# Wv products split by head into 64-column halves, and the first batch's qk splits moved

## The reference, cut to what matters

```python
q = (xn @ w_q).reshape(B, SQ, 16, 64)
k, v = jnp.split(context @ w_kv, 2, axis=-1)
scores = jnp.einsum('bqhd,bkhd->bhqk', q * SCALE, k)
attn = jax.nn.softmax(scores, axis=-1)
out = jnp.einsum('bhqk,bkhd->bqhd', attn, v).reshape(B, SQ, 1024)
out = out @ w_out + b_out
```

## Time and profile before

| | us |
|---|---|
| median of 3 runs | 995.58 |
| lowest, highest | 993.61, 996.96 |
| the profiled execution's time | 992.81 |
| its span | 991.0 |
| PE busy in the span | 942.5 (95%) |
| PE weight loads busy | 815.2 |
| DVE busy | 741.7 |
| ACT busy | 502.8 |
| POOL busy | 561.3 |
| mean granted TensorE clock | 0.993 |

### The profile page before, as it was taken

How to read it: one execution, slowest core, us unless ns; L and a number is a source line. 1 busy time by engine, 2 the same in 40 slices (tenths; PEclk the granted TensorE clock), 3 DMA queues, 4 the chain that set the end, 5 groups by cost and what they waited for, 6 DMA issues and landing times.

```text
span 991.0 us, 17563 instructions
## 1 busy us (share of the span) xinstructions
PE 942.5 (95%) x5732; PEld 815.2 (82%) x5732; DVE 741.7 (75%) x1167; ACT 502.8 (51%) x856; POOL 561.3 (57%) x593
## 2 busy tenths in 40 slices
PE   6898999999999999999999999999998699999998
PEld 3467898888988889888888888998886587888887
DVE  5549787787877878778777887865776666888776
ACT  3447556655565556556555655654452343434432
POOL 5719678668948957876894795720000431444440
PEclk9999999999999999999999999999999799999999
DMA  5872112212211212221221121101004022222200
GB/s 159 274 232 71 45 55 62 56 42 59 63 38 53 71 36 59 60 59 38 60 66 39 47 69 41 54 4 64 1 1 170 1 85 86 86 85 85 85 1 22
DMA packets 75094, 66.50 MB, mean 67 GB/s; under 512 B 7920, under 2 KB 71680, under 8 KB 75008
## 3 DMA queue, kind: packets, MB, share of 16 engines
q1 hardware_dynamic: 75008, 65.37, 21.9%
HBM read 57.48 MB, written 7.86 MB: 66 GB/s over the span
## 4 chain that ended last, share of the span: by engine, by line
PE 83%; DVE 10%; issue 3%; ACT 2%; POOL 2%; DMA 0%; SPq 0%; POOLq 0%; DVEq 0%; ACTq 0%
PE sps L1205 26%; PE scp L1223 9%; PE scp L1224 9%; PE scp L1225 9%; PE scp L1413 5%; PE sps L1399 5%; PE wps L1399 4%; PE wps L1249 3%; PE scp L1414 2%; DVE u_sb L916 2%; DVE st L881 1%; PE sps L1316 1%; PE scp L1173 1%; PE sps L1336 1%; PE sps L1159 1%
## 5 line engine op out<-in xcount | busy, mean ns | idle before, releaser
L1223 PE MATMUL scp<-cn,pt_hi 128*128 128x258 f32 (+1 forms) x832 | 239.7, 288 | 3.6 <-DVE pt_lo L906 2.8
L1224 PE MATMUL scp<-cn,pt_hi 128*128 128x256 f32 (+1 forms) x832 | 234.9, 282 | 0.7 <-issue 0.7
L1225 PE MATMUL scp<-cn,pt_lo 128*128 128x258 f32 (+1 forms) x832 | 234.9, 282 | 0.0
L668 ACT ACTIVATE st<-sps 128x512 f32<-128x512 f32 (+1 forms) x208 | 123.1, 594 | 155.9 <-PE sps L1205 155.1
L906 DVE TENSOR_TENSOR pt_lo<-st,pt_hi 128x512 fp32r<-128x512 f32 (+1 forms) x208 | 194.7, 936 | 6.6 <-ACT pt_hi L677 6.6
L881 DVE TENSOR_TENSOR st<-st,mbc 128x512 f32<-128x512 f32 (+1 forms) x208 | 156.9, 754 | 44.7 <-ACT mbc L691 37.5
L1205 PE MATMUL sps<-qk_hi,ct_hi 128*128 128x512 f32 (+1 forms) x416 | 167.9, 404 | 17.7 <-DVE cmax L892 7.4
L674 ACT ACTIVATE st<-st 128x512 f32<-128x512 f32 (+1 forms) x208 | 130.2, 626 | 93.5 <-DVE st L881 92.7
L1223 PEld LDWEIGHTS scp<-cn,pt_hi 128*128 128x128 f32 (+1 forms) x832 | 156.9, 189 | 13.8 <-DVE pt_lo L906 5.7
L1205 PE MATMUL sps<-qk_hi,ct_lo 128*128 128x512 f32 (+1 forms) x416 | 164.2, 395 | 0.0
L1205 PE MATMUL sps<-qk_lo,ct_hi 128*128 128x512 f32 (+1 forms) x416 | 163.4, 393 | 0.0
(11 more groups left out here) (213 smaller groups left out, 1481.4 us busy)
## 6 DMA issues: line engine op xcount, KB each, us to landing
w_raw<-W SPq DMA_DIRECT2D x16, 1024.0 KB, 7.5
raw<-ctx_t SPq DMA_DIRECT2D x96, 128.0 KB, 2.2
raw<-ctx_n SPq DMA_DIRECT2D x96, 128.0 KB, 2.0
raw<-qk_scratch SPq DMA_DIRECT2D x56, 128.0 KB, 2.0
qk_scratch<-stage_b SPq DMA_DIRECT2D x4, 896.0 KB, 4.6
qk_scratch<-stage_a SPq DMA_DIRECT2D x4, 896.0 KB, 4.5
wq_sb<-w_q SPq DMA_DIRECT2D x1, 1024.0 KB, 5.1
wkt_sb<-w_kt SPq DMA_DIRECT2D x1, 1024.0 KB, 8.0
```

What stands on the lines that cost most here:

```text
L668: act.activation(st[0:rows(j), par, j, :], sps[0:rows(j), u % 2, :], ACT.Copy).then_inc(out_ok, 1)
L1223: pe.matmul(scp[:, t, 0:D + 2], hi, cn[0:rows(j), j, 0:D + 2], start=j == 0, stop=False)
L1224: pe.matmul(scp[:, t, 0:D], hi, cn[0:rows(j), j, D + 2:CNW], start=False, stop=False)
L1225: ins = pe.matmul(scp[:, t, 0:D + 2], lo, cn[0:rows(j), j, 0:D + 2], start=False, stop=j == SJ - 1)
```

## The change

`times_wv` does one product per head and half of the features instead of one for two heads: 64 columns of Wv against that head's 64 columns of u. Head 0's result lands on partitions 0 to 63, head 1's on 64 to 127, both in the same 64 columns of PSUM, so `take_o` is one copy of 128 partitions x 256 instead of two of 64 x 256.

In the first batch `first_high` and `first_low` of tiles 0 to 3 now stand before `q_high` and `q_low` of the next q tile instead of behind them; those of tiles 4 to 7 stand one slot later, behind the next slot's work.

```diff
@@ ScalarE (VectorE the same, with first_low and q_low)
             for t in range(GT):
                 take_qk(t)
+                first_high(t)
                 q_high(GT + t)
-                first_high(t)
@@
                 slot(0, u, u)
                 if u in LATE_TILE:
                     take_qk(LATE_TILE[u])
-                    first_high(LATE_TILE[u])
+                if u - 1 in LATE_TILE:
+                    first_high(LATE_TILE[u - 1])
@@ VectorE, take_o
-                v = wps[:, 0, :].rearrange("p (t q) -> p t q", t=GT)
-                dve.tensor_copy(oT[0:Q, ts_, tok], v[0:Q, :, 0:Q])
-                dve.tensor_copy(oT[Q:P, ts_, tok], v[Q:P, :, Q:P]).then_inc(o_ok, 1)
+                dve.tensor_copy(oT[:, ts_, tok],
+                                wps[:, 0, 0:GT * Q].rearrange("p (t q) -> p t q", t=GT)).then_inc(o_ok, 1)
@@ TensorE, times_wv
                     for dt in range(DT):
-                        ins = pe.matmul(wps[:, 0, t * P:(t + 1) * P], wv_sb[:, dt, h0:h0 + P], ut_sb[:, t, dt, :],
-                                        start=dt == 0, stop=dt == DT - 1)
+                        for hr in head_rows:
+                            ins = pe.matmul(wps[hr, 0, t * Q:(t + 1) * Q],
+                                            wv_sb[:, dt, h0 + hr.start:h0 + hr.stop], ut_sb[:, t, dt, hr],
+                                            start=dt == 0, stop=dt == DT - 1)
```

More of the change, by code:

```diff
@@ L868, in _ @@
                 take_qk(t)
+                first_low(t)
                 q_low(GT + t)
-                first_low(t)
             def rows(j):
@@ L948, in _ @@
                     take_qk(LATE_TILE[u])
-                    first_low(LATE_TILE[u])
+                if u - 1 in LATE_TILE:
+                    first_low(LATE_TILE[u - 1])
             with dve.Fori(0, NPASS - 1) as i:
```

## The result

The changed kernel takes 981.35 us (median of 4 runs, 980.75 to 982.35) against 994.6 us for the kernel before on the same chip (4 runs). The ratio is 0.9872 with a 95% interval from 0.9854 to 0.9889: 13.2 us less. The forecast was 11.5 us less and 984.1 us, with a range of 976.5 to 999. Of the 2.7 us between forecast and result, 1.0 come from the kernel before, whose median is 994.6 over four runs where three had given 995.6; 1.7 are gain that the sum did not have. The profiled execution has a span of 979.0 us, 12.0 less than before.

The account below looks back on a forecast made before the run. TensorE was taken to bound the kernel, except in the first batch, where VectorE and ScalarE steps hold it. Gains 1.6 + 2.5 + 7.4 = 11.5 us, so 995.6 - 11.5 = 984.1 us; range 976.5 to 999.

Parts of the forecast that it names:

- Wv: Each group's Wv products on TensorE go from 1.79 to 1.33 us, 7.4 us less in 16 groups.
- the shape: Entering and leaving column halves around a group's Wv products costs 0.40 us, bounds 0 and twice that.
- main term: Wv products: two heads on different column halves load and multiply at the same time, 7.4 us less in 16 groups.
- staggered in program order: Wv starts: one head's first instruction runs beside the other's second, so four instructions take 116 ns.
- take_o: VectorE's single copy saves 0.42 us a group, 6.7 us in all, hidden beside TensorE and counted as 0.
- Tiles 0 to 3: First batch: with the splits moved ahead, the first scores start at 34.2, gain 1.6 us, bounds 0 to 1.79.
- Tiles 4 to 7: First batch, late tiles: moving first_high lets the maximum end 0.6 us sooner, four times, 2.5 us; some 0.5 us stall stays.
- half-clock stretches: Tail: an earlier arrival can shorten or lengthen time at half clock, adding some 2 us to either side.

Follow-up runs that it names:

- e4: Changed kernel with the Wv loops swapped, head outermost, so four instructions of one head follow each other: 980.06 us, Wv products 1.32 us a group.
- e3: Changed kernel with both heads' Wv products on the same column half and two copies in take_o: 995.47 us, ratio 1.0002.
- e5: Changed kernel with each group's Wv products in two stretches, before and behind the slot's twelve context products: 986.10 us.
- e7: Changed kernel with take_o as two copies of 64 partitions x 256 again, Wv split kept: 980.71 us.
- e2: Kernel before with only the two moves of the qk splits, Wv products as before: 991.09 us.
- e8: Changed kernel with the late tiles' take_qk also one slot later, behind the next score copy and maximum: 978.14 us.
- e6: Changed kernel with the splits of tiles 4 to 7 put back directly behind take_qk, tiles 0 to 3 still moved: 983.84 us.
- e1: Kernel before with only the Wv split and the single copy in take_o, qk splits not moved: 985.43 us.
- e9: Changed kernel with 64 loaded columns but all 128 columns of u moved, take_o of the kernel before: 992.69 us.
- e11: The changed kernel run again unchanged, for direct comparison and spread: 981.58 us.

## Why the prediction was right

**Wv, 7.4 us predicted.** The two column halves do load and multiply at the same time. The group's products went from 1.79 to 1.28 us against 1.33 forecast: 0.93 us for the pairs, as forecast, and 0.35 for the shape, where 0.40 was taken. That is 8.2 us in 16 groups. The mechanism of the main term held. One step under it fell, and it is luck that the number came out all the same: starts are not staggered in program order between the heads. That order gives 116 ns for four instructions, and so do two independent halves at 58 ns a pair, so the forecast could not tell them apart; e4 did. The rule of the Trainium skill, "TensorE: Matmul & The Clock Gate", Part 3, The mechanism, that loads overlap products in flight only with another row group, does not hold in this kernel: both heads use all 128 rows, and e3, on one column half, still has 58 ns a product with loads that are 138 ns long. What the Trainium skill's "TensorEngine Tiling (Array Packing)", Key Properties, states fits these runs: tiles work independently (e3 against the changed kernel), and a change of the tiling mode drains the engine (0.34 us in e5; that the time goes into draining no run here shows).

**take_o, 0 predicted.** e7 agrees.

**Tiles 0 to 3, 1.6 us predicted.** The wait ahead of the first scores fell from 1.79 to 0.13 us, 1.66 us. In e2, where the clock rises at nearly the same time as before, the scores start at 34.54 us, 1.3 us earlier than before; the forecast said 34.2. There the last `first_low` took 0.76 us, where the forecast had 0.42:

```profile
33.68 0.76 DVE L859 TENSOR_TENSOR qk_lo<-stage_a,qk_hi 128x256 fp32r<-128x256 f32 x1 [0.54 <-ACT qk_hi L648]
```

It takes 0.76 to 0.85 us in e2, e7 and e8, where TensorE waits 0.5 us, and at most 0.48 us in the other eight profiled executions with this move, where it waits 0.11 to 0.15. Why it is longer in some executions stays open.

**Tiles 4 to 7, 2.5 us predicted.** From the first scores to those behind the last late tile are 57.38 - 35.09 = 22.3 us. Before, by the same view, they were 60.49 - 35.82 = 24.7 us. That is 2.4 us, and e6 puts it at 2.5. What stays at each of the four tiles is 0.4 us by the view of waits and 0.66 by the periods (5.23 against e8's 4.57); the forecast said 0.5. The forecast held DVE's stage copies to be late next; it was ACT's copies, and e8 takes them away.

**What the sum left out, about 2 us.** The starts of the first and the last transposed maximum enclose the middle of the kernel, with 14 groups' Wv products. In this order: before, in e2, after and in e1:

```profile
L1259 PE MATMUL wps<-ident,cmax x64: 270/272/273, 69.6 to 682.9; 128*128 128x128 f32 x64
```

```profile
L1261 PE MATMUL wps<-ident,cmax x64: 270/272/273, 66.0 to 679.8; 128*128 128x128 f32 x64
```

```profile
L1262 PE MATMUL wps<-ident,cmax x64: 270/272/273, 66.5 to 670.3; 128*128 128x128 f32 x64
```

```profile
L1260 PE MATMUL wps<-ident,cmax x64: 270/272/273, 70.4 to 675.3; 128*128 128x128 f32 x64
```

613.3 and 613.8 us with the old products, 603.8 and 604.9 with the new: 9.2 us less, where 14 x 0.51 are 7.1. Most of the surplus of 2.1 us lies at two places, the turns of the loop over passes, at 340 and 510 us. In the nine profiled executions with the gain of the column halves (all but before, e2, e3 and e9) the two groups there are 1.3 to 2.6 us longer in sum than the groups beside them, with the old products (before, e2) 3.0 to 3.6. It varies between executions of one kernel too: 1.3 for the changed kernel, 1.9 in e11. e3 and e9, whose products are on column halves but slower than before, have 1.5 to 1.6, so it does not come from the time saved. Why the turn is cheaper with this instruction stream was not tested and stays open.

Against this stand the 0.9 us of the slower beginning. From the last transposed maximum to the end are 308.1 us before and 308.7 after. The two remaining groups' gain is in it, but a longer time at half clock goes with the loss of it. The last Wv products start at

```profile
L1249 PE MATMUL wps<-ut_sb,wv_sb x256: 272/275/275, 126.4 to 761.2; 128*128 128x128 f32 x128
```

```profile
L1251 PE MATMUL wps<-ut_sb,wv_sb x512: 222/222/270, 123.1 to 747.1; 128*64 128x64 f32 x171
```

Up to there the tail is 1.4 us shorter (78.2 and 76.9 us), behind it 2.0 us longer (229.8 and 231.8). This last part holds the half-clock stretches of which the forecast warned, with a granted clock of 0.50 (1.2 GHz): 13.7 us of them before, 17.1 after. Over the 13 profiled executions it takes 229.8 to 230.6 us in the seven with 13.7 us at half clock, 231.2 to 231.8 in the five with 17.1, and 233.0 in the one with 20.5 (e3). So the profiled 12.0 us are 3.1 up to the first transposed maximum, 9.5 from there to the last and -0.6 in the tail.

## What to carry to other kernels

When products need only a part of the array's columns, put the parts on different column halves and cut the moving operand too: either cut alone gained nothing here, on one half both together gained nothing, and both on two halves took the products from 1.79 to 0.93 us. Each way there and back costs 0.35 us on top, so such products belong in one stretch. To judge such a change before it runs, read spacings of consecutive starts and find what sets them, because the lengths of instructions hide it. In a chain of copies between engines, move what the bounding engine does not wait for behind what it waits for, and look again afterwards: the next copy in line (e8) was worth another 2.5 to 3 us.

## What the runs showed of the hardware

- Two halves of the columns run loads and products side by side, also when the program gives four instructions of one half and then four of the other (1.32 us against 1.28). 64 instructions, loads counted, start within 0.93 us, 15 ns each; down to that their number was no limit, since a pair on two halves keeps the 58 ns of a single product on one (e3).
- Changing between full array and column halves costs 0.34 to 0.35 us there and back, near the 0.38 of row halves.
- The first rise of the granted clock to its upper level (2.4 GHz) comes between 13.8 and 17.0 us over the 13 profiled executions, with the same code ahead of it, and the first qk product starts between 19.3 and 21.0 us.
- In the tail, 3.4 us more at half clock (17.1 instead of 13.7 us) go with some 1 to 2 us more of time behind the last Wv products.
